# Two-layer transformer block with MoE: q and k rows packed to 81, stepped q loads, ones by DMA, separate staging of batch 1

## What is computed

```python
mod = silu(c) @ w_adaln + b_adaln                      # six rows of 144 per batch
h = modulate(ln(x), sh_msa, sc_msa)
qkv = (h @ w_qkv + b_qkv)                              # 16 heads of 9
attn = softmax(einsum('bhqd,bhkd->bhqk', q, k) * 9 ** -0.5)
x = x + g_msa * ((attn @ v) @ w_proj + b_proj)
xn = modulate(ln(x), sh_mlp, sc_mlp)
# layer 0: top 2 of 4 experts, softmax over their logits as weights cw
eo = gelu(xn @ w1[e] + b1[e]) @ w2[e] + b2[e]          # hidden size 576
x = x + g_mlp * sum_e cw[e] * eo[e]
# layer 1: one MLP of hidden size 576 in place of the experts
```

## Time and profile before

| | us |
|---|---|
| median of three runs | 464.79 |
| lowest and highest of them | 460.39 and 464.89 |
| the profiled execution, its own time | 465.79 |
| its span in the trace | 463.9 |
| TensorE busy (84% of the span) | 390.6 |
| VectorE busy (69%) | 321.0 |
| ScalarE busy (47%) | 216.8 |
| GpSimd busy (18%) | 85.7 |

### The profile page before, as it was taken

How to read it: one execution, slowest core, us unless ns; L and a number is a source line. 1 busy time by engine, 2 the same in 40 slices (tenths; PEclk the granted TensorE clock), 3 DMA queues, 4 the chain that set the end, 5 groups by cost and what they waited for, 6 DMA issues and landing times.

```text
span 463.9 us, 5953 instructions
## 1 busy us (share of the span) xinstructions
PE 390.6 (84%) x1938; PEld 167.9 (36%) x1938; DVE 321.0 (69%) x837; ACT 216.8 (47%) x428; POOL 85.7 (18%) x95
## 2 busy tenths in 40 slices
PE   1616592689999999899999998998998999998897
PEld 0102220112333332337676663651332333322464
DVE  7797283989889888352716852789797788881653
ACT  1113320157777668752243333124676677687421
POOL 5999945990000000000000000000000000000000
PEclk9999955569999999999999999996999999999999
DMA  6000775124741300000000024300023300000001
GB/s 171 1 0 9 177 182 132 34 81 126 205 131 50 81 1 3 0 1 0 2 0 1 0 76 128 104 2 0 1 70 114 102 27 2 0 3 0 1 0 52
DMA packets 19470, 24.05 MB, mean 52 GB/s; under 512 B 5652, under 2 KB 16088, under 8 KB 19116
## 3 DMA queue, kind: packets, MB, share of 16 engines
q1 hardware_dynamic: 15008, 21.47, 16.4%
q0 software_dynamic: 3040, 1.62, 1.7%
q10 hardware_dynamic: 1392, 0.59, 0.4%
...
...
## 4 chain that ended last, share of the span: by engine, by line
PE 62%; DVE 16%; DMA 8%; issue 5%; SPq 4%; ACT 4%; DVEq 0%; ACTq 0%
PE bank L1243 12%; PE bank L1121 12%; PE bank L1258 10%; PE bank L1267 8%; PE bank L1221 8%; DVE nmax L938 6%; DMA Qs<-qk_parts 4%; SPq L475 2%; PE bank L1168 2%; DMA qk_parts<-prob 2%; ACT prob L1072 2%; PE bank L1285 2%; PE bank L1224 2%; DVE mpart L739 2%; DMA w<-in_L_cond_b_adaln_dram 1%
## 5 line engine op out<-in xcount | busy, mean ns | idle before, releaser
L938 DVE TENSOR_REDUCE nmax<-bank 128x1 f32<-128x512 f32 x256 | 165.2, 682 | 35.9 <-PE bank L1258 35.1
L1072 ACT ACTIVATE prob<-bank 128x512 f32<-128x512 f32 x256 | 135.5, 602 | 44.1 <-PE bank L1267 43.5
L1258 PE MATMUL bank<-Ks,Qs 96*128 96x512 bf16 x256 | 103.9, 419 | 19.6 <-DMA Qs<-qk_parts 13.1
L1267 PE MATMUL bank<-Qs,Ks 98*128 98x512 bf16 x256 | 98.3, 397 | 5.4 <-ACT prob L1072 4.2
L1121 PE MATMUL bank<-prob,Va 128*32 128x512 f32 x512 | 71.7, 633 | 0.2
L1258 PEld LDWEIGHTS bank<-Ks,Qs 96*128 96x128 bf16 x256 | 25.1, 100 | 91.6 <-DVE nmax L938 48.7
L1243 PE MATMUL bank<-w,big 128*128 128x144 f32 (+1 forms) x320 | 52.5, 305 | 0.2
L1061 ACT ACTIVATE big<-bank 128x512 f32<-128x512 f32 (+1 forms) x46 | 27.0, 597 | 47.0 <-PE bank L1224 46.9
L1243 PEld LDWEIGHTS bank<-w,big 128*128 128x128 f32 (+1 forms) x320 | 42.6, 188 | 10.6 <-DVE y L904 2.6
L1267 PEld LDWEIGHTS bank<-Qs,Ks 98*128 98x128 bf16 x256 | 25.2, 100 | 36.9 <-ACT prob L1072 16.5
L1221 PE MATMUL bank<-hTb,w 128*128 128x512 f32 x72 | 37.0, 594 | 0.0
...
## 6 DMA issues: line engine op xcount, KB each, us to landing
Ks<-qk_parts SPq DMA_DIRECT2D x30, 108.0 KB
Qs<-qk_parts SPq DMA_DIRECT2D x90, 36.0 KB
...
Qs<-qk_parts SPq DMA_DIRECT2D x18, 108.0 KB
...
```

What stands on the lines that cost most here:

```text
L938: V.tensor_reduce(nmax[:, half, odd * NT + k:odd * NT + k + 1], bank[:, :], AX.X, ALU.max, negate=True).then_inc(s_free, 1)
L1072: A.activation(probs[:, k % 2, j, :], bank[:, :], ACT.Exp, scale=SCALE).then_inc(t_free, 1)
L1258: M.matmul(bank[:, :], Qs[b][0:MROW, h_, k4 * P:(k4 + 1) * P], Ks[b][0:MROW, h_, :], start=True, stop=True).then_inc(s_full, 1)
L1267: M.matmul(bank[:, :], Ks[b][0:SROWS, h0 + k4, k * P:(k + 1) * P], Qs[b][0:SROWS, h0 + k4, :], start=True, stop=True).then_inc(t_full, 1)
```

## The change

- `MROW` goes from 96 to 81: the maxima and the ones stand in rows 81 and 82. There are no zero rows, so the contraction is over 81 rows in the max pass and 83 in the slots, and the fills by GpSimd are gone, with the semaphore `buf_ready`.
- The ones in rows 81 and 82 of Ks come by two DMAs that ScalarE issues at the start, from a small tile of ones in `prob`. TensorE and ScalarE wait for them (`ones_in`).
- A pair of q's part i, k's part j and dimension d stood in row 27i + 9j + d; it now stands in row 27i + 3d + j. Ks is still loaded by three DMAs of 27 rows, in that order. Qs is loaded by three DMAs of 27 rows, one for each j, into every third row, in place of nine of 9 rows.
- Batch 0 is loaded in three pieces: heads 0 to 3, 4 to 7 and 8 to 15.
- Batch 1 of layer 0 is staged in Qs[1], not in `prob`, and ScalarE doesn't wait for the write of batch 0.
- Va[1] is filled by GpSimd before the masks are made. The weights are split in pieces of at most 576 columns.
- The first `ada` of layer 1 comes before `ln` and `qkv` of the first batch, the other two right behind that `qkv`.

```diff
--- before.py
+++ after.py
@@ -39,7 +39,7 @@
 SCALE = HD ** -0.5
 PARTS = 3
 PAIRS = PARTS * PARTS * HD
-MROW = 96
+MROW = PAIRS
 MPARTS = 2
 SROWS = MROW + MPARTS
 G = 4
@@ -73,8 +73,8 @@
 
 
 
-    s = [("ada", 0, 0), ("ln", 0, 0), ("ada", 0, 1), ("ada", 0, 2), ("turn", 0, 0, "a"), ("ln", 0, 1),
-         ("qkv", 0, 0, 0, QKV), ("turn", 0, 1, "a"), ("ada", 1, 0), ("ada", 1, 1), ("qkv", 0, 1, 0, QKV), ("ada", 1, 2)]
+    s = [("ada", 0, 0), ("ln", 0, 0), ("ada", 0, 1), ("ada", 0, 2), ("turn", 0, 0, "a"), ("ada", 1, 0),
+         ("ln", 0, 1), ("qkv", 0, 0, 0, QKV), ("ada", 1, 1), ("ada", 1, 2), ("turn", 0, 1, "a"), ("qkv", 0, 1, 0, QKV)]
     s += [("max", 0, u) for u in range(UNIT_LEAD)]
     for l in range(L):
         n0 = B * l
@@ -120,7 +120,7 @@
 
 
 
-PIECES = (((0, G), (G, NH)), tuple((h, h + G) for h in range(0, NH, G)))
+PIECES = (((0, G), (G, 2 * G), (2 * G, NH)), tuple((h, h + G) for h in range(0, NH, G)))
 PIECES_AT = (((0, 1), (0, 3), (1, 1), (1, 3)), ((2, 0), (2, 1), (2, 3), (3, 1)))
 
 
@@ -338,8 +338,10 @@
         wraw = big[0:ROWS, 0:WN]
 
 
+        onesb = prob[0:MPARTS, 0:N // 2].bitcast(BF16)
+
         qkf, qkp = [], []
-        for place in (prob, prob, prob, big):
+        for place in (prob, Qs[1][:, :, :].rearrange("p h n -> p (h n)").bitcast(F32), prob, big):
             qkf.append(place[:, 0:3 * N].rearrange("p (c n) -> p c n", c=3))
             qkp.append(place[:, 3 * N:3 * N + 9 * N // 2].bitcast(BF16)
                        .rearrange("p (c i n) -> p c i n", c=3, i=PARTS))
@@ -371,7 +373,8 @@
         ld_w = [sem(f"ld_w{l}") for l in range(L)]
 
         c_ready = sem("c_ready")
-        buf_ready = sem("buf_ready")
+        ones_ready = sem("ones_ready")
+        ones_in = sem("ones_in")
         v_ready = [sem(f"v_ready{b}") for b in range(B)]
 
         s_full, s_free = sem("s_full"), sem("s_free")
@@ -460,19 +463,17 @@
                 for n, piece in pieces_after(stage):
                     b, parts = n % B, qk_dram[n]
                     sp.wait_ge(qk_out[n], 4 * 16)
-                    if n < B:
-                        sp.wait_ge(buf_ready, n + 1)
-                    else:
+                    if n >= B:
                         sp.wait_ge(t_full, scores_ended(n - B))
                     lo, hi = PIECES[b][piece]
-                    width, cols, done = (hi - lo) * N, slice(lo * N, hi * N), qk_in[n][piece]
-                    src = parts[1].rearrange("j (d h) n -> (j d) (h n)", h=NH)[:, cols]
-                    for r in range(0, PAIRS, HD * PARTS):
+                    cols, done = slice(lo * N, hi * N), qk_in[n][piece]
+                    src = parts[1].rearrange("j (d h) n -> d j (h n)", h=NH)[:, :, cols]
+                    for i_ in range(PARTS):
+                        r = HD * PARTS * i_
                         sp.dma_start(Ks[b][r:r + HD * PARTS, lo:hi, :], src).then_inc(done, 16)
-                    for i_ in range(PARTS):
-                        src = parts[0, i_].rearrange("(d h) n -> d (h n)", h=NH)[:, cols]
-                        for r in range(HD * PARTS * i_, HD * PARTS * (i_ + 1), HD):
-                            sp.dma_start(Qs[b][r:r + HD, lo:hi, :], src).then_inc(done, 16)
+                    src = parts[0].rearrange("i (d h) n -> (i d) (h n)", h=NH)[:, cols]
+                    for j in range(PARTS):
+                        sp.dma_start(Qs[b][j:PAIRS:PARTS, lo:hi, :], src).then_inc(done, 16)
                 if stage[0] == "ada" and stage[1:] != (0, 0):
 
                     _, l, part = stage
@@ -540,6 +539,8 @@
                 return G_.tensor_tensor(stk, raw, stk, ALU.add)
 
             load_raw("qkv0")
+            link(G_.memset(Va[1][:, :, :, :], 0.0))
+            G_.memset(Va[1][:, :, :, HD:HD + 1], 1.0).then_inc(v_ready[1], 1)
             G_.memset(mask1[:, :], -1.0)
             G_.memset(mask2[:, :], -1.0)
             G_.memset(ident[:, :], 0.0)
@@ -560,24 +561,16 @@
             split_weights(*WCOLS["qkv0"]).then_inc(w_split, 1)
             pool.wait_ge(w_split, 1)
 
-            pair_of_ones = 0x3F803F80
-            for b in range(B):
-                G_.memset(Qs[b][64:96, :, :].bitcast(I32), 0)
-                link(G_.memset(Ks[b][64:96, :, :].bitcast(I32), 0))
-                G_.memset(Ks[b][96:SROWS, :, :].bitcast(I32), pair_of_ones).then_inc(buf_ready, 1)
-                pool.wait_ge(buf_ready, b + 1)
-                if b == 0:
-                    link(G_.memset(Va[1][:, :, :, :], 0.0))
-                    G_.memset(Va[1][:, :, :, HD:HD + 1], 1.0).then_inc(v_ready[1], 1)
-                    pool.wait_ge(v_ready[1], 1)
             for name in sources:
                 if name != "qkv0":
                     load_raw(name)
 
             pool.wait_ge(ld_raw[1], 16 * (5 * 3 + 3 * E + 5 * 3))
-            for k, (name, last) in enumerate((("proj0", "gate"), ("w1", "w1"), ("qkv1", "fc1"))):
-                a = WCOLS[name][0]
-                split_weights(a, sum(WCOLS[last]) - a).then_inc(w_split, 1)
+            for name, last in (("proj0", "gate"), ("w1", "w1"), ("qkv1", "fc1")):
+                a, end = WCOLS[name][0], sum(WCOLS[last])
+                for at in range(a, end, HID):
+                    done = split_weights(at, min(HID, end - at))
+                done.then_inc(w_split, 1)
 
         @block.vector
         def _(dve):
@@ -776,6 +769,7 @@
                 V.tensor_tensor(x[:, b], x[:, b], y[:, :, :], ALU.add).then_inc(x_ready, 1)
 
 
+            V.memset(onesb, 1.0).then_inc(ones_ready, 1)
             for r in BIAS_ROWS:
                 V.memset(stN[:, :, r:r + 1], 1.0)
             V.memset(ones[:, :], 1.0)
@@ -980,6 +974,10 @@
                           allow_slow_non_contiguous=True).then_inc(ld_c, 16)
             act.dma_start(cTr[:, :], t["cond_1152"][:, P:C].rearrange("b c -> c b"),
                           allow_slow_non_contiguous=True).then_inc(ld_c, 16)
+            act.wait_ge(ones_ready, 1)
+            for b in range(B):
+                act.dma_start(Ks[b][MROW:SROWS, :, :],
+                              onesb.unsqueeze(1).to_broadcast([MPARTS, NH, N])).then_inc(ones_in, 16)
 
             for i, stage in enumerate(SCHED):
                 kind, t_at = stage[0], T_AT[i]
@@ -1018,7 +1016,9 @@
                 elif kind == "qkv":
                     _, l, b, first, last = stage
                     n = B * l + b
-                    if n and first == 0:
+                    if n == 0:
+                        act.wait_ge(ones_in, 16 * B)
+                    if n > 1 and first == 0:
                         act.wait_ge(qk_out[n - 1], 4 * 16)
                     if n == B:
                         act.wait_ge(p_used, NT * B * HG)
@@ -1064,7 +1064,7 @@
                     _, n0, g, k = stage
                     done = NT * (HG * n0 + g) + k
                     if g == 0 and k == 0:
-                        act.wait_ge(qk_out[1 if n0 == 0 else B], 4 * 16)
+                        act.wait_ge(qk_out[n0], 4 * 16)
                     for j in range(G):
                         bank = take(t_at + j)
                         if done >= 2 and j == 0:
@@ -1253,13 +1253,15 @@
                         b = n % B
                         for piece, (lo, _) in enumerate(PIECES[b]):
                             if k4 == 0 and h_ == lo:
-                                pe.wait_ge(qk_in[n][piece], 16 * (PARTS + PARTS * PARTS))
+                                pe.wait_ge(qk_in[n][piece], 16 * 2 * PARTS)
                         bank = fill_s(s_at + k4 - first)
                         M.matmul(bank[:, :], Qs[b][0:MROW, h_, k4 * P:(k4 + 1) * P], Ks[b][0:MROW, h_, :],
                                  start=True, stop=True).then_inc(s_full, 1)
                     if kind == "slot":
                         _, n0, g, k = stage
                         b, h0 = g // HG, G * (g % HG)
+                        if n0 == 0 and g == 0 and k == 0 and k4 == 0:
+                            pe.wait_ge(ones_in, 16 * B)
                         if k == 0 and k4 % 2 == 0:
                             pair = (NH * n0 + G * g + k4) // 2
                             pe.wait_ge(m_in[pair % 4], 16 * (pair // 4 + 1))
```

## The result

| | before | after |
|---|---|---|
| median of the runs, us | 463.45 (460.39 to 464.89) | 441.85 (439.17 to 444.08) |
| profiled execution, us (span) | 465.79 (463.9) | 440.88 (439.0) |
| ratio, 95% interval | | 0.954 (0.946 to 0.962) |
| busy TensorE, VectorE, ScalarE, GpSimd, us | 390.6, 321.0, 216.8, 85.7 | 393.6, 300.0, 217.1, 69.7 |

The account below looks back on a forecast made before the run. Nearly all TensorE idle time was placed before about 107 us, in fills stalling VectorE, the write and the loads. 26.5 to the first slot + 2.0 + 1.0 - 0.5 = 29.0 off 465.8 gave 436.8, stated as 436 us, range 429 to 445.

Parts of the forecast that it names:

- Fills gone: Before the first qkv matmul: VectorE no longer stands still behind GpSimd's fills, so it starts at 23.0, not 39.17: 16.2 us.
- The write: Split q and k to DRAM: still 6.3 us behind its last issue, since GpSimd's DMAs move forward too; lower bound 3.9.
- The loads: First loads of q and k: six DMAs a piece issue faster than twelve; 0.7 us gained, bounds 0 and 2.2.
- Rival C: Slower: the stepped load of 27 rows runs on one DMA engine instead of nine; 500 us or more, chance 0.03.
- Ones by DMA: At the start: the ones' DMAs share engines with the loads TensorE starts on; 1.0 us late, bounds 0 and 2.3.
- The max pass: Up to the first slot: fifth head's 8.4 us stall goes, `mpart` waits 1.7 instead of 4.0; 26.5 us ahead in all.
- First slots: First slot's matmul to fourth slot's product: long VectorE waits and half the clock's loss go; 2.0 us, bounds 0 and 5.
- Layer 1: TensorE's two waits for layer 1's loads: half a microsecond shorter each; 1.0 us gained, bounds 0 and 3.8.
- `mT` rows: Before the first slot: the first `mT` row DMA queues behind loads and second write; 0.5 us lost, bounds 0 and 3.
- A: Loads come late again, sharing engines with the second write; first slot at 68 to 71, total 441 to 444, chance 0.12.
- B: VectorE is not freed, its long copies being slow for another reason than the fills; about 455 us, chance 0.04.
- D: More is won: upper clock through the max pass, write and loads at their lower bounds; 427 us, chance 0.11.

Follow-up runs that it names:

- e_fills_back: Kernel after with six fills of the old size put back on GpSimd, on rows nothing reads: 460.75 us, ratio 0.991.
- e_after_again: Kernel after, nothing changed, timed again: 441.02 us, ratio 0.953.
- e_after_ref: Kernel after, nothing changed, timed as a reference: 441.5 us, ratio 0.951.
- e_loads_again: Kernel after with the old plain loads of q and k, twelve DMAs a piece, and the ones' DMAs issued later: 438.76 us, ratio 0.948.
- e_combined: Kernel after with the old stage order, the ones' DMAs issued later and weight splits of 288 columns: 440.77 us, ratio 0.952.
- e_two_pieces: Kernel after with batch 0 loaded in two pieces, heads 0 to 3 and 4 to 15: 442.4 us, ratio 0.953.
- e_big_splits: Kernel after with the raw weights split in pieces of up to 2304 columns instead of 576: 446.27 us, ratio 0.966.

## Why the prediction was right, and where it was too low

Its sign, its place and its mechanism held; the size was 5.9 us off. 4.1 of these are the sum (24.9 between the two profiled executions where 29.0 was forecast), the other 1.8 come from where the medians happened to lie beside the profiled executions (0.8 + 1.0). Step by step:

1. **Fills gone: 16.2 forecast, 15.8 found** (first qkv matmul at 23.34, forecast 23.0). e_fills_back shows that it is the fills: 14.8 us come back at this place. The split of the first qkv ended 11.2 us behind that matmul, not 10.3.
2. **The write** landed 4.0 us behind its last issue; I had kept 6.3, with 3.9 as a bound. The bound was the right value: +2.3 that I had not counted. What failed is "They move forward with it (15.5 to 39), so I keep 6.3". GpSimd's DMAs moved forward by 22.5 us and the write by 15, so the twelve large ones of `w`, issued from 44.3 to 51.6 with the write at 48.3, are now issued from 21.8 to 28.6 with the write at 33.3; the small ones that are left beside it do not slow it so. From the forecast's 24.0 for the first qkv matmul (23.0 and the 1.0 of step 4) the sum runs: matmul 0.7 early, split 0.9 longer, write 2.3 shorter, so the first load is issued at 39.0 and not at 41.0.
3. **The loads: 0.7 forecast, 0.0 found.** From first issue to first score matmul it was 7.2 us and is 7.2. The failed piece is "4 heads are issued in about 2.1 us instead of 4.3": it took the duration of a plain DMA's issue (0.33) for a DMA of another pattern. They take 0.72 to 0.85 us each, so six cost more than twelve did. On the transfer itself the first load says little: from first issue to first score matmul it took 7.0 to 9.9 us in the kernels with stepped rows and 7.2 to 10.3 in those with plain ones. Rival C did not come about.
4. **Ones by DMA: 1.0 late forecast, 0.7 found** (10.58 against 9.86). But TensorE's wait for this load was 9.8 and 10.2 in e_after_again and e_after_ref, and 9.6 and 9.5 in e_loads_again and e_combined, where the ones come later: it is somewhere between nothing and 1.0.
5. **The max pass: 10.3 forecast** (26.5 less 16.2), **10.1 found** (27.6 less 17.5). The sum held, its parts only partly. The stall's 8.4 us are gone, but the third piece took only 2.4 of them: e_two_pieces has 2.42 us without it. The `mpart` term was "1.7 instead of 4.0" and measured 2.3 (1.31 + 0.95) instead of 4.2. What the short splits are worth was undersized at 2.3: the weight split now runs from 42 us and meets both pairs ahead of the first slot, so long ones would cost 7.6 and not 4 (e_big_splits, some 5 us on the total).
6. **First slots: 2.0 forecast, 0.9 found.** Here I had hoped for half of the clock's loss. TensorE was granted its lower clock from 43 to 77 us, and before from 57 to 101, so the slots up to the fourth product still ran at 1.2 GHz.
7. **Layer 1: +1.0 forecast, -2.6 found**, the largest miss. Half a microsecond shorter each was taken with step 3's shorter issue, and with that wrong the sign turned: the waits are 2.60 and 2.32 where they were 1.69 and 2.08 in the kernel before. Of the 2.6, some 1.3 are likely the row of windows below, 6.8 us at the lower clock behind the second wait, against 3.4 in the kernel before. The longer wait does not explain it: e_loads_again waits 2.06 there and has the 6.8 us too, e_two_pieces waits 2.73 and has 3.4. So this part of the miss can be luck of the execution.
8. **`mT` rows: 0.5 forecast, 1.0 found**, at 94.25 and not at the first slots. This DMA stands in SyncE's queue behind the six load DMAs of a piece, 4.5 us of issue. That this is its cause is not shown: the same kernel has 0.18 us of it in e_after_ref and none in e_after_again.

Windows of the kernel after (us, then busy time of PE, PEld, DVE, ACT, POOL; granted clock, DMA share, GB/s):

```profile
46.10:62.80 16.70, 14.27 (x27) 2.82 (x28) 15.97 (x27) 0.53 (x2) 15.40 (x18) 0.50 0.55 172
...
77.40:90.00 12.60, 12.60 (x75) 4.30 (x73) 10.96 (x23) 9.70 (x21) 2.56 (x3) 1.00 0.41 118
...
330.00:337.00 7.00, 7.00 (x25) 2.54 (x24) 3.56 (x9) 2.73 (x6) 0.00 (x0) 0.53 0.28 95
```

That the sum is only 4.1 off owes something to luck: up to the first slot the forecast is 1.1 too low, since the write's 2.3 outweighed the terms that were too high, and steps 6 to 8 are 5.2 too high. With the write as forecast the sum would have missed by 6.4.

Rivals: A's price (441 to 444) is near the result, but its mechanism is absent, since the first slot runs at 62.8 and not at 68 to 71. B is refuted by the 0.2 us rows, D by the clock of 0.50 in the max pass, though its lower bound for the write came true.
